# Attention in one fused post-norm block: the value sums of two key tiles issued back to back in the first query chunk

## The chip, the cores and the metric

The kernel runs on one core of a Trainium2 chip. The metric is the device time of one execution in microseconds (us), taken as the median of three runs. Smaller is better.

## What is computed

The reference is one transformer block with layer norms behind both halves. Its input is x, 4096 rows of 256 floats.

```
proj = quant4(x) @ ternary_weight(Wqkv).T + b
q = proj as (16 heads, 4096, 16);  k, v = proj read as (16, 4096, 16) in another order
q, k = rotary(q), rotary(k);   ql, kl = q @ U, k @ U
y = softmax(ql @ kl^T / 4) @ v            # for each head, 4096 x 4096
x1 = layernorm(x + quant4(y) @ ternary_weight(Wo).T)
h = silu(x1 w1) * (x1 w2);  h = gelu(h h1);  h = gelu(h h2)
out = layernorm(x1 + h w3)
```

The softmax is taken without subtracting a row's true maximum; a bound is folded into the scores, and a slower second attempt exists in the program for inputs on which that fails. It isn't run here.

## The kernel before, in words

**Work.** The attention is cut into 8 query chunks of 512 queries and, in each, 4 blocks of 4 heads. A block goes over 32 key tiles of 128 keys. One key tile for the 4 heads of a block is a **unit**, so a block has 32 units, a query chunk 128, and the whole attention 1024. The first query chunk is units 0 to 127.

**One unit** is three steps on three engines' worth of work:

- *Scores* (TensorE, `first_scores_pe`, L722): two **pairs**, each of two matmuls (one per head, 49 rows of contraction, 512 queries), which write two banks of PSUM. There are three such slots (`SLOTS`), used in turn by the pairs, so pair p + 3 can be computed only when pair p has been read.
- *Exponentials* (ScalarE, `first_act`, L812): one activation per pair, 128 x 1024, from PSUM into the ring `PB` of six places (`RING`).
- *Value sums* (TensorE, `first_sums_pe`, L752): 4 matmuls, one per head, with 17 columns of weights (16 values and a one), which add to one bank of PSUM, `ACC`. [...] The last one frees two places of `PB` (`probs_free`).

At the end of a block VectorE transposes `ACC` into `accS` (L1027) and divides; TensorE waits for that (`acc_saved`) ahead of the next block's first sums.

**Order.** TensorE's order is written out by hand in `first_pe`. For each unit: the scores of the pairs three ahead, each behind a wait for the activation that frees its slot; then at most one **setup step**; then the unit's value sums.

```
                for pair in IN_UNIT[unit]:
                    if pair + SLOTS < len(ACT_PAIRS):
                        pe.wait_ge(at["probs_ready"], pair + 1)
                        first_scores_pe(pe, at, pair + SLOTS)
```

**Setup steps.** Keys and queries of later rows are prepared in the gaps of the first chunk. The table `SETUP_AT` says at which unit which step stands: `XT` (L464) and `PR` (L469) turn and project a group of 512 rows, `KT` and `QT` (both L475) turn the rotated keys and queries, `KG` (L479) multiplies keys by U, `KN` and `QN` (L484) take norms, `KM` (L487) turns a maximum. All of them share one bank of PSUM, the last, and each waits until VectorE has read the one before it (`setup_read`). In units 6 to 127 they stand at these units:

- KT and KT at 16 and 17, 34 and 35, 48 and 49, 66 and 67, 80 and 81; KG and KG at the two units behind each of these pairs (18 and 19, 36 and 37, 50 and 51, 68 and 69, 82 and 83)
- PR and PR at 10 and 11, 42 and 43, 74 and 75, 25 and 26, 57 and 58
- KN then XT at 22 and 23, 40 and 41, 54 and 55, 72 and 73; KN alone at 7 and 86; XT alone at 9; KM at 24, 56 and 88
- QT and QT at 98 and 99, 108 and 109, 118 and 119; QN at 103, 113 and 123

KT, KG and KG's second step belong to one group of rows; units 1 and 2 hold a KT each and units 3 and 4 a KG each. ScalarE puts one more activation (`sqk` L526 or `sqq` L531) into its order behind the unit two behind the second KG or QT.

**Later chunks.** From block 7 on, in four units of each block half of the exponentials are made by VectorE (L823 to L839); the sums of these late units stand behind the sums or scores of other units (`LATE_AT`). That of unit 25 of a block stands directly behind the sums of unit 30. After the attention come the output projection and the feed-forward part.

Of the kernel before, what the change touches and what calls it, by code (L numbers as in the profile page):

```python
# [22 lines left out]
KT = N // P  # L23
# [8 lines left out]
NBLK = H // BL  # L32
# [57 lines left out]
LATE_NUMBER = {_u: _k for _k, _u in enumerate(LATE)}  # L90
# [45 lines left out]
def postln_block(nc, a, out):  # L136
    ctx = ExitStack()
    with ctx:
# [569 lines left out]
        def first_scores_pe(pe, at, pair):  # L708
            unit, s = ACT_PAIRS[pair]
            b, kt = divmod(unit, KT)  # L710
            q, k = divmod(unit, KQ)
            if s == 0 and k == 0:
                pe.wait_ge(at["k_in"][q % 2], keys_in(at, 0, q))
                if q < 2:
                    pe.wait_ge(consts_first[q], 64)
            if unit == 0 and s == 0:
                pe.wait_ge(q_first, 64)
            elif s == 0 and kt == 0:
                pe.wait_ge(at["q_in"][b % 2], (b // 2 + b % 2) * 64)
            for e in range(2):  # L720
                r = slice(64 * e, 64 * e + at["rows"])
                ins = pe.matmul(PS[:, 2 * (pair % SLOTS) + e, :], KSL[r, q % 2, s, k * P:(k + 1) * P],  # L722
                                QSL[r, b % 2, s, :], start=True, stop=True, tile_position=(64 * e, 0))
            ins.then_inc(at["scores_ready"], 1)

        def late_scores_pe(pe, at, unit, e):

            n = LATE_NUMBER[unit]
            b = unit // KT
            q, k = divmod(unit, KQ)  # L730
            pe.wait_ge(at["k_in"][q % 2], keys_in(at, 0, q))
            if n == 0 and e == 0:
                pe.wait_ge(setup_read, len(USE))
            else:
                pe.wait_ge(poly_read, 2 * n + e)
            r = slice(64 * e, 64 * e + at["rows"])
            pe.matmul(MISC, KSL[r, q % 2, 1, k * P:(k + 1) * P], QSL[r, b % 2, 1, :], start=True, stop=True,  # L737
                      tile_position=(64 * e, 0)).then_inc(poly_scores, 1)

        def first_sums_pe(pe, at, unit):  # L740
            hb, kt = unit // KT % NBLK, unit % KT
            c, u = divmod(kt, HT)
            if unit in LATE_NUMBER:
                pe.wait_ge(poly_ready, LATE_NUMBER[unit] + 1)
            pe.wait_ge(at["probs_ready"], IN_UNIT[unit][-1] + 1)
            for i in range(BL):
                h = hb * BL + i
                if unit in LATE_NUMBER:
                    probs = (late_act, late_dve)[i // 2][LATE_NUMBER[unit] % 2]
                else:  # L750
                    probs = PB[:, (2 * IN_RING[unit] + i // 2) % RING, :]
                ins = pe.matmul(ACC[i * VW:i * VW + DK + 1, :], V17[:, HT * h + u, c, :],  # L752
                                probs[:, (i % 2) * QW:(i % 2 + 1) * QW],
                                start=kt == 0, stop=kt == KT - 1, tile_position=(0, i * VW))
            ins.then_inc(late_free if unit in LATE_NUMBER else at["probs_free"], 1)

        def first_pe(pe, at):
            def place(unit, n):
                for what, late in PLACES.get((unit, n), []):
                    if what == "sums":  # L760
                        first_sums_pe(pe, at, late)
                    else:
                        late_scores_pe(pe, at, late, what)

            pe.wait_ge(setup_read, len(BEFORE))
            for pair in range(SLOTS):
                first_scores_pe(pe, at, pair)
            visits = {FIRST_Y: ("Y", 0)}
            for k in range(2):
                visits[FIRST_O[k]], visits[FIRST_X[k]] = ("O", k), ("X", k)  # L770
            for unit in range(NB_ALL * KT):
                place(unit, 0)
# [4 lines that stand above are left out]
                    if pair == IN_UNIT[unit][0]:  # L777
                        place(unit, 1)
                if unit in SETUP_AT:
                    setup_pe(pe, *SETUP_AT[unit])  # L780
                n = unit - KT * (NB_ALL - 1)
                if n == FIRST_Y:
                    pe.wait_ge(poly_read, 2 * len(LATE))
                if n in visits:
                    first_chunk_pe(pe, *visits[n], 0)
                if n == FIRST_W:
                    pe.wait_ge(fx1T_split, 2)
                    pe.wait_ge(least_weight, 1)
                    pe.transpose(MISC[0:1, 0:P], sm[:, 5, 1:2], ident[:, :]).then_inc(weights_T, 1)
                place(unit, 2)  # L790
                if unit % KT == 0:
                    pe.wait_ge(at["acc_saved"], unit // KT + 1)
                if unit not in LATE_NUMBER:
                    first_sums_pe(pe, at, unit)
                place(unit, 3)

        def first_act(act, at):
# [121 lines left out]
        def first_chunk_pe(pe, what, k, r):  # L919
            if what == "Y":  # L920
                pe.wait_ge(fy_ready, r + 1)
                for i in range(TQ):
                    for c in range(DC):
                        ins = pe.transpose(MISCB[:, i * DC + c, :], first_qb[:, i, c * P:(c + 1) * P], identb[:, :])
                ins.then_inc(fyT_ready, 1)
            elif what == "O":
                pe.wait_ge(fyT_saved, r + 1)
                if k:
                    pe.wait_ge(fo_read, 2 * r + 1)
                for i in range(2):  # L930
                    for c in range(DC):
                        ins = pe.matmul(MISC[:, i * D:(i + 1) * D], qTb[:, (2 * k + i) * DC + c, :], sgn[:, 1, c, :],
                                        start=c == 0, stop=c == DC - 1)
                ins.then_inc(fo_ready, 1)
            else:
                pe.wait_ge(fx1_ready, r + 1)
                if k:
                    pe.wait_ge(fx1T_split, 2 * r + 1)
                for i in range(TQ):
                    ins = pe.transpose(MISC[:, i * P:(i + 1) * P], yq[:, i, k * P:(k + 1) * P], ident[:, :])  # L940
                ins.then_inc(fx1T_ready, 1)
# [648 lines left out]
        def _(pe):  # L1590
# [22 lines left out]
            for v in BEFORE[1:]:  # L1613
                setup_pe(pe, *v)
            first_pe(pe, first)
            def again_pe(pe):
                maxima_pe(pe)
# [154 lines left out]
```

## Time and profile before

| What | Value |
|---|---|
| Median of 3 runs | 2587.75 us (2587.68 to 2589.11) |
| Profiled execution, its own time | 2590.94 us |
| Span of the trace | 2589.1 us |
| TensorE (matmul) busy | 2516.6 us, 97% |
| ScalarE busy | 2014.8 us, 78% |
| VectorE busy | 1740.3 us, 67% |
| First activation of the attention | at 66.72 us |
| Mean granted clock of TensorE | 0.991 of full speed |

Times in the trace count from the start of its span, and the profiled execution's own time is 1.8 us longer than that span. TensorE's matmuls overlap, so its share of busy time is no measure of how close it is to its limit. A row of a timeline merges neighbouring instructions of one kind: its start, its length from the first start to the last end, the count, and in brackets the idle time of that engine just ahead, with what ended it.

### The profile page before, as it was taken

How to read it: one execution, taken by the hardware profiler on the slowest of the kernel's cores; microseconds unless marked ns; L12 is line 12 of the kernel's file. 1: busy time of each engine (PE TensorE's matmuls, PEld its weight loads, DVE VectorE, ACT ScalarE, POOL GpSimd, SP SyncE). 2: the span in 40 equal slices, each digit the busy share in tenths (PEclk: the TensorE clock that was granted, in tenths of full speed). 3: DMA queues.
4: the chain of work that ended last, by engine and by line, in shares of the span. 5: the costliest groups of instructions: out<-in, count | busy, mean ns of one | idle time of the engine just before them, and what ended most of it. 6: DMA issues, size and time to landing. Idle time of an engine off the chain costs nothing.

```text
span 2589.1 us, 41403 instructions
## 1 busy us (share of the span) xinstructions
PE 2516.6 (97%) x15898; PEld 1094.7 (42%) x15898; DVE 1740.3 (67%) x2485; ACT 2014.8 (78%) x2230; POOL 40.4 (2%) x77
## 2 busy tenths in 40 slices
PE   3999999999999999999999999999999999999998
PEld 2222222222222222222222222222248888888886
DVE  7454345787787787887777877777644566646563
ACT  2899999999999999999999999999962223222232
POOL 1000001100000000000000000000100000000000
PEclk8999999999999999999999999999999999999999
DMA  3543447833343333243333334333630101110000
GB/s 106 122 103 88 109 115 158 167 62 70 59 77 71 68 64 71 58 76 71 66 65 71 59 75 73 63 68 72 122 63 1 25 0 24 24 24 16 8 8 18
DMA packets 100192, 172.27 MB, mean 67 GB/s; under 512 B 31208, under 2 KB 56840, under 8 KB 100014
## 3 DMA queue, kind: packets, MB, share of 16 engines
q1 hardware_dynamic: 89166, 151.84, 29.2%
q0 software_dynamic: 9120, 16.18, 3.1%
q8 instruction: 112, 1.84, 0.3%
q10 hardware_dynamic: 1728, 1.87, 0.3%
q14 instruction: 66, 0.54, 0.1%
HBM read 144.31 MB, written 25.49 MB: 66 GB/s over the span
## 4 chain that ended last, share of the span: by engine, by line
PE 85%; ACT 6%; issue 5%; DVE 3%; DMA 1%; ACTq 0%; SPq 0%; DVEq 0%
PE PS L752 33%; PE PS L722 24%; PE PS L1284 18%; ACT PB L812 5%; PE PS L1269 5%; PE PS L1296 2%; PE PS L737 2%; ACT EXP L812 1%; PE PS L475 1%; PE PS L479 1%; DMA wh1r<-in_mlp 0%; DVE yq L848 0%; DVE same L850 0%; PE PS L484 0%; PE PS L469 0%
## 5 line engine op out<-in xcount | busy, mean ns | idle before, releaser
L812 ACT ACTIVATE PB<-PS 128x1024 f32<-128x1024 f32 x1856 | 1734.5, 1139 | 38.0 <-PE PS L722 35.2
L752 PE MATMUL PS<-PB,V 128*17 128x512 f32 x7424 | 979.8, 600 | 3.5 <-DVE accS L1027 2.6
L722 PE MATMUL PS<-QSL,KSL 49*128 49x512 f32 x3904 | 838.0, 469 | 19.2 <-ACT PB L812 11.6
L722 PEld LDWEIGHTS PS<-QSL,KSL 49*128 49x128 f32 x3904 | 351.3, 184 | 937.5 <-ACT PB L812 851.0
L835 DVE SCALAR_TENSOR_TENSOR EXP<-EXP 128x1024 f32<-128x1024 f32 x288 | 352.8, 1225 | 9.9
L1363 ACT ACTIVATE hfr<-PS,s 128x512 f32<-128x512 f32 x128 | 86.9, 690 | 300.3 <-PE PS L1284 300.2
L752 PEld LDWEIGHTS PS<-PB,V 128*17 128x17 f32 x7424 | 123.2, 95 | 284.0 <-issue 217.4
L823 DVE TENSOR_SCALAR EXP<-PS 128x512 f32<-128x512 f32 x192 | 132.6, 691 | 157.0 <-PE PS L737 154.5
L1284 PE MATMUL PS<-hidden_ar,wh1r 128*128 128x512 f32 x1024 | 237.5, 391 | 0.0
L1284 PE MATMUL PS<-hidden_br,wh2r 128*128 128x512 f32 x1024 | 235.3, 390 | 0.0
L1284 PEld LDWEIGHTS PS<-hidden_br,wh2r 128*128 128x128 f32 x1024 | 191.7, 188 | 39.4
L1284 PEld LDWEIGHTS PS<-hidden_ar,wh1r 128*128 128x128 f32 x1024 | 190.7, 188 | 40.1 <-DVE hfr L1456 0.5
L1355 ACT ACTIVATE SLr<-PS,s 128x512 f32<-128x512 f32 x64 | 44.2, 691 | 122.1 <-PE PS L1269 122.1
L1269 PE MATMUL PS<-x1Tr,w12r 128*128 128x512 f32 x512 | 122.9, 400 | 2.3 <-issue 2.3
L1390 DVE CAST hidden_br<-hfr 128x512 fp32r<-128x512 f32 x64 | 27.3, 426 | 138.2 <-ACT hfr L1363 138.2
L832 DVE TENSOR_TENSOR EXP<-EXP 128x1024 f32<-128x1024 f32 x96 | 117.6, 1225 | 3.3
L839 DVE SCALAR_TENSOR_TENSOR EXP<-EXP 128x1024 f32<-128x1024 f32 x96 | 117.7, 1226 | 3.3
L827 DVE SCALAR_TENSOR_TENSOR EXP<-EXP 128x1024 f32<-128x1024 f32 x96 | 117.6, 1225 | 3.3
L1390 DVE CAST hidden_ar<-hfr 128x512 fp32r<-128x512 f32 x128 | 54.6, 426 | 94.8 <-ACT hfr L1363 92.5
L812 ACT ACTIVATE EXP<-PS 128x1024 f32<-128x1024 f32 x96 | 109.8, 1144 | 0.0
L1027 DVE STREAM_TRANSPOSE accS<-PS 128x512 f32<-128x512 f32 x32 | 22.9, 717 | 127.0 <-PE PS L752 126.7
L1269 PEld LDWEIGHTS PS<-x1Tr,w12r 128*128 128x128 f32 x512 | 94.1, 192 | 28.7 <-DVE hfr L1456 7.4
(184 smaller groups left out, 1463.8 us busy)
## 6 DMA issues: line engine op xcount, KB each, us to landing
KSL<-KSD SPq DMA_DIRECT2D x255, 256.0 KB
KSL<-KSD SPq DMA_DIRECT2D x255, 128.0 KB
QSD<-qhl SPq DMA_DIRECT2D x32, 256.0 KB
wh2r<-in_mlp POOLq DMA_DIRECT2D x32, 256.0 KB, 4.3
QSL<-QSD SPq DMA_DIRECT2D x62, 132.0 KB
KSD<-khl SPq DMA_DIRECT2D x58, 128.0 KB
xg<-in_x SPq DMA_DIRECT2D x8, 512.0 KB, 6.4
y<-Y SPq DMA_DIRECT2D x32, 128.0 KB, 2.2
```

What stands on the lines that cost most here:

```text
L722: ins = pe.matmul(PS[:, 2 * (pair % SLOTS) + e, :], KSL[r, q % 2, s, k * P:(k + 1) * P], QSL[r, b % 2, s, :], start=True, stop=True, tile_ ...
L752: ins = pe.matmul(ACC[i * VW:i * VW + DK + 1, :], V17[:, HT * h + u, c, :], probs[:, (i % 2) * QW:(i % 2 + 1) * QW], start=kt == 0, stop=k ...
L812: act.activation(probs, PS[:, slot:slot + 2, :].rearrange("p a b -> p (a b)"), ACT.Exp).then_inc(at["probs_ready"], 1)
L823: v.tensor_scalar(ey[:, e * QW:(e + 1) * QW], MISC, LOG2E, -126.0, ALU.mult, ALU.max).then_inc(poly_read, 1)
L827: s.did(v.scalar_tensor_tensor(ee, et, TO_WHOLE, ey, ALU.subtract, ALU.subtract))
L832: s.did(v.tensor_tensor(ey, ey, ee, ALU.mult))
L835: s.did(v.scalar_tensor_tensor(ey, ey, POW2[c], ee, ALU.add, ALU.mult))
L839: v.scalar_tensor_tensor(late_dve[k % 2], ey, POW2[0], et, ALU.add, ALU.mult).then_inc(poly_ready, 1)
L1269: ins = pe.matmul(PS[:, 2 * (o % 2) + w, :], w12[:, w, c, o * P:(o + 1) * P], x1p[:, r, c, :], start=c + r == 0, stop=c == DC - 1 and r == ...
L1284: ins = pe.matmul(PS[:, o % 4, :], wh[l - 1][:, c, o * P:(o + 1) * P], hidden[(l - 1) % 2][:, r, c, :], start=c + r == 0, stop=c == HC - 1 ...
L1363: act.activation(hf[:, o % FB, :] if exact else hidden[l % 2][:, 0, o, :], PS[:, o % 4, :], ACT.Gelu, scale=s12[:, 1 + l, o:o + 1]).then_i ...
L1390: sf.did(v.tensor_copy(parts[0], whole))
```

## The change

In units 0 to 127 an even unit issues no value sums. The odd unit behind it issues, after its own scores and its own setup step, the sums of the even unit and then its own. From unit 128 on nothing is changed.

```
                 place(unit, 2)
-                if unit % KT == 0:
-                    pe.wait_ge(at["acc_saved"], unit // KT + 1)
-                if unit not in LATE_NUMBER:
-                    first_sums_pe(pe, at, unit)
+
+                for ready in (unit,) if unit >= NBLK * KT else (unit - 1, unit) if unit % 2 else ():
+                    if ready % KT == 0:
+                        pe.wait_ge(at["acc_saved"], ready // KT + 1)
+                    if ready not in LATE_NUMBER:
+                        first_sums_pe(pe, at, ready)
                 place(unit, 3)
```

No instruction is added or removed, on any engine or queue. Only TensorE's order changes. The diff shifts the lines below it by two, so L812 becomes L814 and L1027 becomes L1029; L722 and L752 keep their numbers.

TensorE at the start of the attention (units 0 to 3; L722 are scores, L752 value sums, L475 and L479 setup steps), as one piece of the difference:

```order
-L722 MATMUL PS<-QSL,KSL 128x512 x10
-L752 MATMUL PS<-PB,V 17x512 x4
-L722 MATMUL PS<-QSL,KSL 128x512 x4
+L722 MATMUL PS<-QSL,KSL 128x512 x14
 L475 MATMUL PS<-ident,rk 128x128 x4
-L752 MATMUL PS<-PB,V 17x512 x4
+L752 MATMUL PS<-PB,V 17x512 x8
 L722 MATMUL PS<-QSL,KSL 128x512 x4
 L475 MATMUL PS<-ident,rk 128x128 x4
```

The sums of unit 0 moved behind the scores and the setup step of unit 1.

TensorE in units 16 to 19, where both KT and both KG steps of a group stand, before:

```order
L722 MATMUL PS<-QSL,KSL 128x512 x4
L475 MATMUL PS<-ident,rk 128x128 x4
L752 MATMUL PS<-PB,V 17x512 x4
L722 MATMUL PS<-QSL,KSL 128x512 x4
L475 MATMUL PS<-ident,rk 128x128 x4
L752 MATMUL PS<-PB,V 17x512 x4
L722 MATMUL PS<-QSL,KSL 128x512 x4
L479 MATMUL PS<-rkT,gblk 128x512
L752 MATMUL PS<-PB,V 17x512 x4
L722 MATMUL PS<-QSL,KSL 128x512 x4
L479 MATMUL PS<-rkT,gblk 128x512
L752 MATMUL PS<-PB,V 17x512 x4
```

and with the change:

```order
L722 MATMUL PS<-QSL,KSL 128x512 x4
L475 MATMUL PS<-ident,rk 128x128 x4
L722 MATMUL PS<-QSL,KSL 128x512 x4
L475 MATMUL PS<-ident,rk 128x128 x4
L752 MATMUL PS<-PB,V 17x512 x8
L722 MATMUL PS<-QSL,KSL 128x512 x4
L479 MATMUL PS<-rkT,gblk 128x512
L722 MATMUL PS<-QSL,KSL 128x512 x4
L479 MATMUL PS<-rkT,gblk 128x512
L752 MATMUL PS<-PB,V 17x512 x8
```

The two KG steps (L479) now have only four score matmuls between them, and 8 sum matmuls (16 records) follow behind the second.

## Rows read from the trace of the kernel before

**Rows 1.** The page: busy time by engine, share of the span, instructions.

```profile
PE 2516.6 (97%) x15898; PEld 1094.7 (42%) x15898; DVE 1740.3 (67%) x2485; ACT 2014.8 (78%) x2230; POOL 40.4 (2%) x77
```

**Rows 2.** Waits, 85 to 331 us: who waited for whom, total, times, longest.

```profile
ACT PB L812 <- PE PS L722: 12.7, 32, 0.8
...
PEld PS L752 <- DVE accS L1027: 0.9, 3, 0.3
```

**Rows 3.** Timeline of ScalarE: start, length, idle time ahead.

```profile
84.43 1.05 ACT L526 ACTIVATE sqk<-khl 128x1024 fp32r<-128x1024 f32 x1
85.38 10.30 ACT L812 ACTIVATE PB<-PS 128x1024 f32<-128x1024 f32 x11
...
250.05 28.51 ACT L812 ACTIVATE PB<-PS 128x1024 f32<-128x1024 f32 x31
```

**Rows 4.** Timeline of TensorE's matmuls, units 18 to 23.

```profile
108.92 0.73 PE L722 MATMUL PS<-QSL,KSL 49*128 49x512 f32 x4
109.58 1.12 PE L479 MATMUL PS<-rkT,gblk 128*128 128x512 f32 x2
110.64 1.05 PE L752 MATMUL PS<-PB,V 128*17 128x512 f32 x8
111.62 0.73 PE L722 MATMUL PS<-QSL,KSL 49*128 49x512 f32 x4
112.28 1.12 PE L479 MATMUL PS<-rkT,gblk 128*128 128x512 f32 x2
...
119.14 0.64 PE L484 MATMUL PS<-sqk,nbk 128*16 128x512 f32 x2
119.70 1.05 PE L752 MATMUL PS<-PB,V 128*17 128x512 f32 x8
```

**Rows 5.** Timeline of VectorE behind a KG, a KN and a KT step.

```profile
108.04 0.69 DVE L618 COPY rkT<-PS 128x512 f32<-128x512 f32 x1 [1.54 <-PE PS L475]
...
111.47 0.69 DVE L630 TENSOR_TENSOR khl<-PS,khl 128x512 fp32r<-128x512 f32 x1
...
119.88 0.68 DVE L638 TENSOR_REDUCE kmp<-PS 16x2 f32<-16x512 f32 x1 [1.52 <-PE PS L484]
```

**Rows 6.** Timeline of TensorE: KT (107 us) and PR (125 us), VectorE's read of PR.

```profile
107.35 0.66 PE L475 MATMUL PS<-ident,rk 128*128 128x128 f32 x4
107.94 1.05 PE L752 MATMUL PS<-PB,V 128*17 128x512 f32 x8
...
125.31 0.61 PE L469 MATMUL PS<-sgn,qTb 128*128 128x256 bf16 x4
125.84 1.05 PE L752 MATMUL PS<-PB,V 128*17 128x512 f32 x8
125.95 0.88 DVE L603 SCALAR_TENSOR_TENSOR xq<-PS,mx,alpha 128x256 f32<-128x256 f32 x2 [1.25 <-PE PS L469]
```

**Rows 7.** Timeline, 276 to 279 us: the second QT step and VectorE's reads.

```profile
276.68 0.65 PE L475 MATMUL PS<-ident,rq 128*128 128x128 f32 x4
...
278.10 0.69 DVE L630 TENSOR_TENSOR qhl<-PS,qhl 128x512 fp32r<-128x512 f32 x1
```

**Rows 8.** Timeline, 846 to 850 us: two units' sums in succession, in a later block.

```profile
846.08 0.50 PE L722 MATMUL PS<-QSL,KSL 49*128 49x512 f32 x2
846.51 1.05 PE L752 MATMUL PS<-PB,V 128*17 128x512 f32 x8
847.38 1.04 PE L752 MATMUL PS<-EXP,V 128*17 128x512 f32 x8
848.35 0.73 PE L722 MATMUL PS<-QSL,KSL 49*128 49x512 f32 x4
...
848.89 1.02 ACT L812 ACTIVATE PB<-PS 128x1024 f32<-128x1024 f32 x1
```

**Rows 9.** Timeline of TensorE, a pair of scores that waits for its slot.

```profile
86.45 0.50 PE L722 MATMUL PS<-QSL,KSL 49*128 49x512 f32 x2
```

**Rows 10.** Busy time by stretch: TensorE, its weight loads, VectorE, ScalarE, GpSimd, granted clock.

```profile
60.00:80.00 20.00, 13.73 (x64) 4.59 (x64) 7.76 (x12) 10.46 (x11) 1.47 (x4) 0.62 0.68 146
```

## The prediction

> **What bounds the kernel now.** I looked first at the busy times. TensorE shows 97% [rows 1], but its matmuls overlap, and the share says little. So I read who waits in the stretch that the change touches, the first query chunk. From 85 us to its end ScalarE waits for scores only 32 times, 12.7 us in all [rows 2]. Between these waits it runs without a break: 31 activations in 28.51 us, so that, with one of 1.02 us, the pitch is (28.51 - 1.02) / 30 = 0.916 us [rows 3]. ScalarE is the bound, and TensorE holds it up only where setup steps make a unit longer than two activations, 1.83 us: a unit with a KG takes 111.62 - 108.92 = 2.70 us [rows 4]. Each break costs ScalarE the gap that is shown and 1.02 - 0.916 = 0.105 us of lost overlap. The chunk before therefore loses 12.7 + 32 x 0.105 = **16.1 us** against an unbroken ScalarE.
>
> **What the change does to the time.** It gives no engine less to do. It makes TensorE's work coarser, and the point is how far ahead of ScalarE the scores are: three PSUM slots, so three pairs. I follow one round of two units (four pairs) from the last pair of scores of the odd unit to the same place in the next round.
>
> - That pair must wait until its slot is read. It starts 0.05 us after an activation's end: 85.38 + 1.02 = 86.40, against 86.45 [rows 3, 9].
> - Sums follow 846.51 - 846.08 = 0.43 us after its start. Two units' sums in succession take 0.87 and 0.97 us until scores start again, 848.35 - 846.51 = 1.84 us [rows 8]. The trace has this order once in each later block, so this is no guess.
> - The next pair of scores feeds an activation 848.89 - 848.35 = 0.54 us after its start. This activation is the one whose end frees the slot for the last pair of the next round. It takes 1.02 us, and 0.05 us later the round is closed.
>
> The round is 0.43 + 1.84 + 0.54 + 1.02 + 0.05 = **3.88 us**. Four activations need 4 x 0.916 = 3.66 us. So a round without any setup step, which costs ScalarE nothing now, will cost **0.22 us**. The cover that it had is gone: a single unit's sums, 111.62 - 110.64 = 0.98 us [rows 4], end 0.6 us before the scores behind them are needed; two units' sums end 0.22 us too late.
>
> A setup step in the *odd* unit stands inside this loop, between the last scores and the sums, and adds all its length. A step in the *even* unit stands beside ScalarE's waiting and adds nothing by itself. But if both units have one, the second needs the shared bank, which VectorE must first have read, and now only four score matmuls stand between the two steps, where sums stood as well. Such a round is counted from its first scores: 0.66 us to the even step (109.58 - 108.92 [rows 4]), then the time until the bank is free, then the odd step, then 1.84 us of sums. The bank is free (VectorE's end plus an estimated 0.09 us for the hand-over; after a KG TensorE goes on at most 0.12 us behind it, 112.28 against 112.16):
>
> - KT: 108.04 + 0.69 - 107.35 = 1.38, so 1.47 us; KN: 119.88 + 0.68 - 119.14 = 1.42, so 1.51; PR: 125.95 + 0.88 - 125.31 = 1.52, so 1.61 [rows 4 to 6].
> - KG, which VectorE reads twice: 111.47 + 0.69 - 109.58 = 2.58, so 2.67; QT likewise 278.10 + 0.69 - 276.68 = 2.11, so 2.20 [rows 4, 5, 7].
>
> The steps' own lengths are 0.59 (KT, and QT taken as that), 0.53 (PR, and XT taken as 0.55), 0.56 (KN) and 1.06 us (KG) [rows 4, 6]. From unit 6 to 127 there are 61 rounds. Their loss against 3.66 us:
>
> - 26 rounds with no step in the odd unit: 26 x 0.22 = 5.7
> - 7 with a short step in the odd unit that finds the bank free (units 7, 9, 25, 57, 103, 113, 123): 7 x (0.22 + 0.55) = 5.4
> - 5 KT with KT: 5 x (0.66 + 1.47 + 0.59 + 1.84 - 3.66 = 0.90) = 4.5
> - 4 KN with XT: 4 x (0.66 + 1.51 + 0.55 + 1.84 - 3.66 = 0.90) = 3.6
> - 3 PR with PR (units 10, 42, 74): 3 x (0.66 + 1.61 + 0.53 + 1.84 - 3.66 = 0.98) = 2.9
> - 3 QT with QT: 3 x (0.66 + 2.20 + 0.59 + 1.84 - 3.66 = 1.63) = 4.9
> - **5 KG with KG**: 5 x (0.66 + 2.67 + 1.06 + 1.84 - 3.66 = 2.57) = 12.9
> - 8 in which ScalarE has an extra activation of 85.38 - 84.43 = 0.95 us (L526, and L531 taken alike) [rows 3]: TensorE's delay is hidden, 0
>
> Together 39.9 us, where 16.1 are lost now: **23.8 us more**.
>
> The rest comes to nothing. In units 0 to 5 TensorE runs at a granted clock of 0.62 in the mean of its 20 us [rows 10]. The scores of unit 1 now come before the first, slow sums, which gains about 1.5 us; the KT and KG steps of units 2 and 3 give it back. I take 0 and keep 2 us on both sides, since the order of the work there could also move the moment at which the clock rises. The three waits for VectorE's transpose at block ends, 0.9 us [rows 2], disappear behind the second unit's scores, but they weren't on ScalarE's path and are worth 0. No DMA moves; the loads of keys are released by counts of scores and get more time, not less. Everything after unit 127 starts later by what the chunk lost.
>
> The profiled execution took 2590.94 us, 3.2 us over the median; the same difference on the median gives 2587.75 + 23.8 = **2611.5 us**.
>
> **A rule weighed.** Sums that follow sums cost 0.87 us where sums before scores cost 0.97 [rows 8]: 0.10 us saved. The Trainium skill, TensorEngine Tiling (Array Packing), Key Properties, says that a change of tiling mode drains TensorE, and scores (two row tiles) and sums (four column tiles) are different modes. The row agrees in direction, and by this rule the change should help; it halves the changes of mode. This case's rows decide what that is worth, below.
>
> **The rivals.**
>
> - *TensorE's work is what counts, and it gets shorter: faster.* If the first sums save 0.10 us and the scores side, for which there is no row, as much again, 64 rounds save 13 us of TensorE's time. What can be won is only where ScalarE waits now: 32 units in which TensorE is never idle, 16 rounds x 0.2 = 3 us, so about 2584; all of it gone would be 2587.75 - 16.1 = 2572. This decides if the sums of two units, with scores ahead and behind, fit into the three pairs of scores in hand, that is if 1.84 us were under 1.62. Rows 8 speak against it, the long chain through TensorE for it. Chance 0.05.
> - *No difference.* The waits gone in the odd positions and the new ones balance, if the KG rounds hide behind VectorE and the plain rounds cost nothing. 2587 to 2592. Chance 0.05.
> - *Slower, but the shared bank isn't felt.* VectorE reads sooner, or the second step stands late enough. Then KG with KG costs 0.66 + 1.06 + 0.66 + 1.06 + 1.84 - 3.66 = 1.62, QT 0.81, and the others 0.75 to 0.81: 8.9 us less, so 2602.7. Chance 0.15.
> - *Slower still.* The clock rises later at the start (2 us), and each of 53 rounds takes 0.05 to 0.1 us more than these rows say (3 to 5 us): 2617 to 2619. Chance 0.15.
>
> The forecast itself has 0.6. The range goes from 2602 to 2619. A measurement of this kernel tells about 0.2%, or 5.2 us, from no change. Faster by more than that 0.05, within it 0.05, slower 0.90.
>
> **What would show it.** In the trace after, between 85 us and the end of the chunk, ScalarE should wait for scores in some 53 places instead of 32; single waits of about 0.1 us in plain rounds (0.22 less the overlap), about 2.4 us at the five KG rounds. Units 16 to 19 should show the second L479 starting about 2.7 us after the first, with TensorE idle near 1 us ahead of it, waiting for VectorE's L630. Each two sets of sums should be 1.84 us. The time from unit 128 on should be unchanged. I am wrong if plain rounds keep 3.66 us, or if the second KG starts directly behind its scores.

## The result and the profile after

| | before | with the change |
|---|---|---|
| Median, first measurement | 2587.72 us | 2616.59 us (2615.83 to 2617.79, 4 runs) |
| Ratio, 95% interval | | 1.011 (1.0095 to 1.0125) |
| Median, second measurement (e9) | 2589.92 us | 2612.83 us (2611.69 to 2614.69, 4 runs) |
| Ratio, 95% interval | | 1.0092 (1.0075 to 1.0108) |
| Profiled execution of the first | 2590.94 us, span 2589.1 | 2617.79 us, span 2616.0 |

The change makes the kernel slower by 28.9 us in the first measurement and by 22.9 in the second. I had said 23.8. TensorE's clock is the likely reason why the two measurements differ; how far that is shown comes below.

The page of the kernel after, as in [rows 1]:

```profile
PE 2514.0 (96%) x15898; PEld 1101.5 (42%) x15898; DVE 1739.9 (67%) x2485; ACT 2019.4 (77%) x2230; POOL 40.1 (2%) x77
```

No engine has more to do. (The records count some matmuls twice: a unit's four matmuls of value sums are 8 records and a KG's one is 2, while the two of a pair of scores are 2.) The waits of ScalarE from 85 us to the end of the first chunk, now at 360 us (who waited for whom, total us, times, longest), answer to [rows 2]:

```profile
ACT PB L814 <- PE PS L752: 26.1, 27, 2.1
ACT PB L814 <- PE PS L722: 6.4, 27, 0.9
```

54 waits instead of 32, and 32.5 us instead of 12.7. Most is put down to the value sums (L752), which free the places of the ring `PB`, and not to the scores. The 54 are two in each of the 27 rounds with a step in the odd unit, one behind sums and one behind scores. The list leaves out the short waits of the plain rounds. They can be seen in ScalarE's timeline, where 18 activations at the pitch would take 17 x 0.916 + 1.02 = 16.59 us:

```profile
132.84 17.50 ACT L814 ACTIVATE PB<-PS 128x1024 f32<-128x1024 f32 x18 [0.18 <-PE PS L722]
```

The 0.91 us beyond that are four plain rounds with 0.23 us each, a gap of about 0.12 us and the lost overlap. TensorE in units 26 to 33, in its timeline (units 28 to 33 have no setup step):

```profile
134.34 1.91 PE L752 MATMUL PS<-PB,V 128*17 128x512 f32 x16
136.19 0.98 PE L722 MATMUL PS<-QSL,KSL 49*128 49x512 f32 x6
137.80 0.49 PE L722 MATMUL PS<-QSL,KSL 49*128 49x512 f32 x2 [0.64 <-ACT PB L814]
138.23 1.91 PE L752 MATMUL PS<-PB,V 128*17 128x512 f32 x16
140.07 0.99 PE L722 MATMUL PS<-QSL,KSL 49*128 49x512 f32 x6
141.69 0.51 PE L722 MATMUL PS<-QSL,KSL 49*128 49x512 f32 x2 [0.63 <-ACT PB L814]
142.12 1.91 PE L752 MATMUL PS<-PB,V 128*17 128x512 f32 x16
```

The loop of the prediction can be read off. The last pair of scores starts at 137.80, the sums 0.43 us later, scores again 1.84 us after that, and the next last pair at 141.69: a round of 3.89 us. TensorE itself waits 0.64 us in each for the slot to be read, and ScalarE 0.12 us for scores: both engines wait for each other in turn. The KG round of units 18 and 19, against [rows 4, 5], first TensorE:

```profile
113.28 1.12 PE L479 MATMUL PS<-rkT,gblk 128*128 128x512 f32 x2
114.34 0.73 PE L722 MATMUL PS<-QSL,KSL 49*128 49x512 f32 x4
115.92 1.12 PE L479 MATMUL PS<-rkT,gblk 128*128 128x512 f32 x2 [0.85 <-DVE khl L630]
116.97 1.91 PE L752 MATMUL PS<-PB,V 128*17 128x512 f32 x16
118.81 0.96 PE L722 MATMUL PS<-QSL,KSL 49*128 49x512 f32 x6
```

then VectorE's read of the bank:

```profile
115.17 0.69 DVE L630 TENSOR_TENSOR khl<-PS,khl 128x512 fp32r<-128x512 f32 x1
```

and ScalarE's activation behind the block:

```profile
118.15 1.02 ACT L814 ACTIVATE PB<-PS 128x1024 f32<-128x1024 f32 x1 [2.14 <-PE PS L752]
```

The second KG starts 2.64 us after the first, behind VectorE's second read, with 0.85 us of idling ahead of it.

I took the length of every round from the ends of its activations (from the last of one round to the last of the next; TensorE works three pairs ahead, so the round of units 6 and 7 is felt in the activations of units 8 and 9). The loss is what goes beyond 3.67 us, four times the pitch, and beyond the extra activation where there is one. Summed over units 6 to 127:

| Rounds | predicted | before | first profile | e9's profile |
|---|---|---|---|---|
| 26 without a step in the odd unit | 5.7 | 0.7 | 5.8 | 5.9 |
| 7 with one short step there | 5.4 | 0.7 | 10.3 | 5.5 |
| 5 KT with KT | 4.5 | 1.8 | 4.6 | 4.6 |
| 4 KN with XT | 3.6 | 1.2 | 3.1 | 3.1 |
| 3 PR with PR | 2.9 | 2.2 | 2.9 | 2.9 |
| 3 QT with QT | 4.9 | 1.1 | 4.8 | 4.8 |
| 5 KG with KG | 12.9 | 8.7 | 12.7 | 12.7 |
| 8 with an extra activation | 0 | -0.2 | -0.2 | -0.2 |
| Sum (rounding apart) | 39.9 | 16.1 | 44.0 | 39.3 |

The waits give the same sum another way: 32.5 us, 54 times 0.105 us of lost overlap, and 26 times 0.22 in the plain rounds are 43.9 us.

Only one line is far off in the first profile, and it is all in three rounds: those of units 102, 112 and 122, with a QN step, lose 2.4 us each and not 0.8. TensorE there, in the first profile:

```profile
302.32 0.50 PE L722 MATMUL PS<-QSL,KSL 49*128 49x512 f32 x2 [0.42 <-ACT PB L814]
302.76 1.02 PE L484 MATMUL PS<-sqq,nbk 128*16 128x512 f32 x2
303.71 3.13 PE L752 MATMUL PS<-PB,V 128*17 128x512 f32 x16
```

and in e9's, the same program executed again:

```profile
301.52 0.50 PE L722 MATMUL PS<-QSL,KSL 49*128 49x512 f32 x2 [0.42 <-ACT PB L814]
301.96 0.64 PE L484 MATMUL PS<-sqq,nbk 128*16 128x512 f32 x2
302.53 1.91 PE L752 MATMUL PS<-PB,V 128*17 128x512 f32 x16
```

The same matmuls take 3.13 us once and 1.91 the other time. The busy times of two stretches (TensorE, its loads, VectorE, ScalarE, GpSimd, then the granted clock), the fall and what came ahead of it in the first profile:

```profile
302.80:306.20 3.40, 3.40 (x16) 0.58 (x18) 2.39 (x4) 1.76 (x3) 0.00 (x0) 0.50 0.93 218
299.00:302.80 3.80, 2.96 (x21) 0.91 (x14) 0.00 (x0) 3.80 (x5) 0.00 (x0) 1.00 0.63 203
```

The granted clock is at half, 1.2 GHz, from 302.8 to 306.2 us, and so twice more. Ahead of it ScalarE runs off its reserve (scores that TensorE made in advance during the extra activation), and TensorE has only single pairs of scores to issue, 0.9 us apart. The cost is (2.40 + 2.41 + 2.43) - 3 x 0.8 = 4.8 us.

The profiled executions differ by 26.9 us. The rounds make 44.0 - 16.1 = 27.9 of it. The first activation came 0.8 us later (67.55 against 66.72), and from there to the end of unit 7 it took 0.15 us more. Units 130 to 135 lose another 0.5 us. Then 1.9 us come back at a block end near 457 us, and 0.8 us behind the attention. At that block end the profile of before shows a fall of the clock (457.7 us), the one after doesn't. The difference to before changes there by 1.6 us in e9's profile and 2.4 in e7's, which have no fall either, and by 0.1 in e4's, which has one at 481.9 us. By these figures the fall cost the profiled execution of before about 2 us, which has nothing to do with the change.

### The profile page after: what moved, and what is told of

It reads as the page before. It is cut to its first block, busy times and chain, and to the rows that moved or that the text cites. A ratio compares the mean times of both kernels' runs of the same rounds, so it can differ in the third digit from the quotient of the medians.

```text
span 2616.0 us, 41403 instructions
## 1 busy us (share of the span) xinstructions
PE 2514.0 (96%) x15898; PEld 1101.5 (42%) x15898; DVE 1739.9 (67%) x2485; ACT 2019.4 (77%) x2230; POOL 40.1 (2%) x77
## 3 DMA queue, kind: packets, MB, share of 16 engines
q8 instruction: 112, 1.84, 0.3%
## 4 chain that ended last, share of the span: by engine, by line
PE 76%; ACT 12%; issue 8%; DVE 3%; DMA 1%; ACTq 0%; POOL 0%; SPq 0%; DVEq 0%; POOLq 0%
PE PS L752 28%; PE PS L722 19%; PE PS L1286 18%; ACT PB L814 11%; PE PS L1271 5%; PE PS L1298 2%; ACT EXP L814 1%; PE PS L737 1%; PE PS L479 1%; PE PS L475 1%; DMA wh1r<-in_mlp 0%; DVE yq L850 0%; DVE same L852 0%; PE PS L469 0%; ACT sqk L526 0%
## 5 line engine op out<-in xcount | busy, mean ns | idle before, releaser
L814 ACT ACTIVATE PB<-PS 128x1024 f32<-128x1024 f32 x1856 | 1740.0, 1140 | 60.6 <-PE PS L752 29.2
L752 PE MATMUL PS<-PB,V 128*17 128x512 f32 x7424 | 970.5, 601 | 3.1 <-DVE accS L1029 2.2
L722 PE MATMUL PS<-QSL,KSL 49*128 49x512 f32 x3904 | 837.9, 469 | 41.4 <-ACT PB L814 33.9
L722 PEld LDWEIGHTS PS<-QSL,KSL 49*128 49x128 f32 x3904 | 352.7, 184 | 930.1 <-ACT PB L814 820.8
L752 PEld LDWEIGHTS PS<-PB,V 128*17 128x17 f32 x7424 | 130.2, 95 | 303.3 <-issue 241.7
L1029 DVE STREAM_TRANSPOSE accS<-PS 128x512 f32<-128x512 f32 x32 | 22.9, 716 | 133.5 <-PE PS L752 133.2
L814 ACT ACTIVATE EXP<-PS 128x1024 f32<-128x1024 f32 x96 | 110.3, 1149 | 0.0
```

The lines of the kernel that those rows point to most:

```text
L814: act.activation(probs, PS[:, slot:slot + 2, :].rearrange("p a b -> p (a b)"), ACT.Exp).then_inc(at["probs_ready"], 1)
```

## Experiments

The experiments ran on three chips. All times are set against the kernel before as measured on the same chip beside them: 2589.02 us for e1 to e4, 2588.65 for e5 to e8, 2589.92 for e9.

**e1: pair only where the odd unit has no step.**

```
-                for ready in (unit,) if unit >= NBLK * KT else (unit - 1, unit) if unit % 2 else ():
+                round_of = unit // 2 * 2
+                paired = unit < NBLK * KT and round_of + 1 not in SETUP_AT
+                for ready in (unit,) if not paired else (unit - 1, unit) if unit % 2 else ():
```

> The sums are paired only in the 34 rounds whose odd unit has no setup step; elsewhere they stand as before. Theory (three pairs of scores in hand, two units' sums end 0.22 us too late): each plain round costs ScalarE 0.22 us, rounds with the extra activation nothing, and where a round ahead of setup steps has lost its reserve the first step there costs up to 0.45 us more; in sum 8.5 us over before, 2596, no drop of TensorE's clock in the first chunk. Rival 1 (every pairing costs alike, 28.9 us / 64 = 0.45 us each): 34 x 0.45 = 15 us, 2603. Rival 2 (fewer changes of tiling mode help, only setup steps hurt): at or under 2587.7, plain rounds at 3.66 us.

Measured: 2596.97 us, 8.0 over before (1.0031, 1.0019 to 1.0044). The 26 plain rounds lose 0.22 or 0.23 each, the 8 rounds with an extra activation nothing, the unpaired KG rounds 1.73 to 1.74 as before, and the KT and QT rounds 0.80 instead of 0.35, the lost reserve. Their sum is 24.7, 8.6 over before, and I had expected 8.5. TensorE goes from the one form to the other in its timeline:

```profile
136.03 0.49 PE L722 MATMUL PS<-QSL,KSL 49*128 49x512 f32 x2 [0.64 <-ACT PB L816]
136.46 1.91 PE L752 MATMUL PS<-PB,V 128*17 128x512 f32 x16
138.30 0.99 PE L722 MATMUL PS<-QSL,KSL 49*128 49x512 f32 x6
139.92 0.51 PE L722 MATMUL PS<-QSL,KSL 49*128 49x512 f32 x2 [0.63 <-ACT PB L816]
```

A round of 139.92 - 136.03 = 3.89 us, without any setup step near. Both rivals fall. With 0.45 us for every pairing it would be 2603 us, which lies above the interval, and 8 of the 34 pairings cost nothing. And where TensorE changes its mode half as often, no round is faster.

**e2: the same pairings, the other parity.**

```
-                for ready in (unit,) if unit >= NBLK * KT else (unit - 1, unit) if unit % 2 else ():
+                for ready in (unit,) if unit >= NBLK * KT - 1 or unit == 0 else (unit - 1, unit) if unit % 2 == 0 else ():
```

> As many pairings as in the change, but a round is an odd unit and the even unit behind it, so that the two KG steps, and the two QT steps, fall into different rounds. Theory: a KT first and a KG second costs 1.37 us, a KG first 0.56 us and that is hidden behind the extra activation, QT with KT's length 0.8 us instead of 1.6; against that the three block ends now fall inside a round (the second sums wait for VectorE's transpose), 1.3 us each instead of 0.22; in sum 16 us over before, 2604, and no clock drop in the QN rounds. Rival (the number of pairings or the doubled sums alone decide, the shared bank does not): the same time as with the change, 2616.6.

Measured: 2607.65 us, 18.6 over before (1.0069, 1.0052 to 1.0086). The change has 28.9 and 22.9; the interval of the second (from 1.0075) still touches this one, so the rounds have to decide. They lose 31.8 us together, against 39.3 in e9's profile, which has no fall of the clock in the attention either. That is 15.7 over before, with 1.25 or 1.26 at each of the three block ends; I had expected 16 in all. The start of the attention loses 2.4 us more (the last activation of unit 7 ends at 89.67 instead of 87.31), which wasn't in my 16. TensorE in units 17 to 20:

```profile
111.26 0.66 PE L475 MATMUL PS<-ident,rk 128*128 128x128 f32 x4
111.85 0.87 PE L722 MATMUL PS<-QSL,KSL 49*128 49x512 f32 x4
112.76 1.13 PE L479 MATMUL PS<-rkT,gblk 128*128 128x512 f32 x2
113.82 1.91 PE L752 MATMUL PS<-PB,V 128*17 128x512 f32 x16
115.66 0.73 PE L722 MATMUL PS<-QSL,KSL 49*128 49x512 f32 x4
116.32 1.12 PE L479 MATMUL PS<-rkT,gblk 128*128 128x512 f32 x2
```

The second KG (116.32) now has a double block of sums ahead of it and no wait for VectorE, and the QT rounds go from 1.59 to 0.81. So the shared bank is one term of the change's price, and the parity decides it.

**e3: late sums, but not in succession.** The edit is shown against the kernel with the change. `sums_of` issues one unit's sums, with its wait.

```
                    if pair == IN_UNIT[unit][0]:
                        place(unit, 1)
+                        if unit < NBLK * KT and unit % 2:
+                            sums_of(unit - 1)
...
-                for ready in (unit,) if unit >= NBLK * KT else (unit - 1, unit) if unit % 2 else ():
+                for ready in (unit,) if unit >= NBLK * KT or unit % 2 else ():
+                    sums_of(ready)
```

> In the odd unit the even unit's sums stand between its two pairs of scores, and its own sums at the end: the sums are as late as in the change but no two follow each other. Theory: what costs is the length of the double block; plain rounds go back to 3.66 us (0 lost), the reserve for a step in an odd unit is 0.15 us instead of 0.65, so setup rounds lose somewhat more than before; in sum 8.5 us over before, 2596. Rival (it is the even unit's late sums, which free the ring of exponentials late): plain rounds lose 0.22 us as in the change, 2610 or more.

Measured: 2597.94 us, 8.9 over before (1.0036, 1.0023 to 1.0048). The plain rounds are back at 0.00 us of loss (0.37 in two that lost 0.35 before), and the rounds with one step in the odd unit lose 0.42 to 0.47 instead of 0.77 (0.18 at unit 9). What costs is the length of the block, not that the even unit's sums come late. They come one pair of scores earlier here than in the change; the ring, which they free, is taken up in e4.

**e4: the change with eight places for exponentials.** The two added places lie in `first_y` and `first_x`, free until unit 972; behind unit 127 there are six again.

```
+        def place_number(n):
+            return n % 8 if n < 2 * NBLK * KT else n % RING
...
-                    if n >= RING:
-                        act.wait_ge(at["probs_free"], (n - RING) // 2 + 1)
-                    probs = PB[:, n % RING, :]
+                    if n in BEFORE_IT:
+                        act.wait_ge(at["probs_free"], BEFORE_IT[n] // 2 + 1)
+                    probs = place_of(n)
```

> The change, with eight places for exponentials instead of six in the first chunk (the two added places lie in tensors that are not used until much later). The profile puts 26 us of ScalarE's waits in the first chunk down to the value sums, which free the ring. Theory (three PSUM slots for scores end the round): these waits go, but the scores are not earlier, so every round keeps its length: 2616.6, within 1 us. Rival (the ring of six is what binds): the waits for sums go and the time falls by 10 to 26 us, 2591 to 2607.

Measured: 2616.98 us, 28.0 over before (1.0109, 1.0092 to 1.0126). Waits of ScalarE in the first chunk:

```profile
ACT PB L829 <- PE PS L722: 17.8, 15, 2.4
ACT first_x L829 <- PE PS L722: 12.8, 12, 2.4
ACT PB L829 <- PE PS L767: 1.7, 1, 1.7
```

27 waits for sums have become one (1.7 us, where the ring shrinks again), and the rounds are where they were: 0.22, 0.92 and 2.53 us of loss, with waits for scores in their place. In its profile every round of the first chunk is within 0.02 us of the same round in e9's, save the last, which loses 1.76 us instead of 0.22 as the ring shrinks. This profiled execution has no fall of the clock in the first chunk and took 2615.27 us. The median lies higher because of two others, which took 2618.7 and 2618.9 us and have no trace. The profile's 26 us "for L752" were true and without consequence. In the change's own KG round the activation held by the ring starts at 118.15 and the next, held by scores, at 119.35: 1.20 us on, 0.28 more than the pitch of 0.92. So the scores would have held the second of the two 0.28 us longer than the ring held the first, and with the ring taken away they still hold the round.

**e5 and e6: where the fall of the clock comes from.** The edit is that of e1 with other conditions: `round_of + 1 not in (99, 101, 109, 111, 119, 121)` and `round_of + 1 not in (103, 113, 123)`.

> The change, but with the sums unpaired in the three rounds with both QT steps and the three rounds behind them (units 98 to 101, 108 to 111, 118 to 121). The change's profile showed TensorE's granted clock fall to half in the QN rounds that follow (3 stretches of 3.4 us, 1.65 us lost in each beyond the ledger). Theory (it is the idling in the QT rounds, where TensorE waits 0.7 us for VectorE and then for ScalarE's extra activation, that brings the clock down): QT rounds lose 0.35 us instead of 1.59, the clock stays up, the QN rounds lose 0.79 us; 3.7 us under the change from the rounds and up to 5 more from the clock: 2608 to 2613. Rival (the drop belongs to the QN round and its doubled sums): the drop stays, QN rounds at 2.4 us.

> The change, but with the sums unpaired in the three QN rounds (units 102 and 103, 112 and 113, 122 and 123). Theory (the drop of the clock comes from what TensorE did ahead of them): the drop is still there, since it begins at the QN step, and the QN rounds lose 1 us or more; the time is 0 to 3 us under the change, 2614 to 2617. Rival (the drop is made by the doubled sums in that round): no drop, these rounds lose nothing, 2.4 x 3 = 7 us under the change, 2609.

Measured: e5 2612.12 us, 23.5 over before (1.0093, 1.0078 to 1.0109), e6 2609.16 us, 20.5 over before (1.0079, 1.0063 to 1.0094). In e5's profile the QT rounds lose 0.80 each (not 0.35, since the plain round ahead had used up the reserve, as in e1), and the clock still falls in two of the three QN rounds, which lose 2.2 and 2.4 us. My theory that the waits in the QT rounds bring it down is refuted. e6's profile has no fall in the attention, and its QN rounds lose nothing. That fitted the rival, but e9 takes the proof away again.

**e9: the change once more.**

> The change itself once more, on the chip that runs it now. Open is whether TensorE's drop to half clock in the QN rounds (4.9 us beyond the ledger in the first profile; absent in the profile of the change with a ring of eight) comes in every execution. Theory (it comes in some, as the QN rounds leave TensorE with single pairs of scores for some 3 us and the drop depends on how they fall): executions spread over about 5 us, those with a mean granted clock of 0.991 or more near 2612 to 2615, those of 0.990 and less near 2616 to 2619. Rival (it is fixed in the order of the work): all within 1 us of 2617, with the same clock.

Measured: 2612.83 us, 22.9 over before, and in its profile no fall of the clock in the attention; this is the program whose first profile had three. So the fall comes in one execution and not in another. In e9 the stretch ahead of the QN step has the same busy times as the one that I showed above:

```profile
298.00:301.80 3.80, 2.96 (x20) 0.86 (x12) 0.00 (x0) 3.80 (x5) 0.00 (x0) 1.00 0.63 194
301.80:305.20 3.40, 3.40 (x26) 0.97 (x24) 2.57 (x5) 2.82 (x4) 0.00 (x0) 1.00 0.87 224
```

2.96 us of TensorE and 3.80 of ScalarE in 3.80, in both. I found nothing in the rows that tells the two apart. The theory on e9 was borne out in that executions can differ, but not in that they spread within one measurement: all four of e9 were alike (2611.69 to 2614.69, mean clock 0.991 and 0.992), and all four of the first lie above them (2615.83 to 2617.79, 0.989 to 0.991). The rival, all near 2617, is refuted. A difference between chips isn't excluded by this, but e4's four, on one chip, fell into 2613.5 and 2615.3 with 0.991 and 2618.7 and 2618.9 with 0.990. What decides it stays open.

**e7 and e8: a version that beats both.** Without pairing, only the sums of a unit with a KG step go behind the first pair of scores of the next unit, and the first QT step stands two units earlier.

The edit is shown against the kernel before:

```
-    SETUP_AT.update({_u: (QT_, 0, _g), _u + 1: (QT_, 1, _g), _u + 5: (QN, 0, _g)})
+    SETUP_AT.update({_u - 2: (QT_, 0, _g), _u + 1: (QT_, 1, _g), _u + 5: (QN, 0, _g)})
...
+            late_sums = {u for u, v in SETUP_AT.items() if v[0] == KG}
...
                    if pair == IN_UNIT[unit][0]:
                        place(unit, 1)
+                        if unit - 1 in late_sums:
+                            sums_of(unit - 1)
...
+                if unit not in late_sums:
+                    sums_of(unit)
```

e8 has in addition other units for the steps (XT, PR, PR, KT, KT, KG, KG, KN): 8, 11, 12, 16, 17, 18, 19, 22, then 23, 25, 26, 30, 32, 35, 37, 40, then 41, 43, 44, 48, 49, 50, 51, 54, then 57, 58, 60, 64, 65, 67, 68, 72, then 74, 75, 76, 80, 81, 82, 83, 86.

> A version of the kernel before that uses what was learned: no pairing. Only the sums of a unit with a KG step are moved behind the first pair of scores of the next unit, so that the long step no longer delays that pair; and the first QT step of a group stands two units earlier, so that the reserve grows back between the two. Theory (what counts is how early the next scores are, three pairs in hand): the rounds with KG lose 1.3 us instead of 1.73, the QT rounds nothing instead of 0.35 (seven of them, four behind unit 127); 4.3 us under the kernel before, 2584 to 2585. Rival (later sums free the ring later, or more changes of mode cost TensorE more): no gain, or slower by 1 to 3 us.

> As the run before it, and the steps of the later groups of rows are spread further apart (a unit without a step between the PR, KT and KG steps where their order allows it). Theory: another 2.2 us from the reserve that grows back by 0.18 us in each unit without a step; 6.5 us under the kernel before, 2582 to 2583. Rival: VectorE, whose chain between the steps gets less time, makes TensorE wait, and the gain is lost.

Measured: e7 2584.51 us, 4.1 under before (0.9983, 0.9974 to 0.9992); e8 2582.24 us (2581.89 to 2583.6, 9 runs), 6.4 under before (0.9976, 0.9966 to 0.9985). In e8, TensorE in units 18 and 19:

```profile
109.35 1.12 PE L479 MATMUL PS<-rkT,gblk 128*128 128x512 f32 x2
110.41 0.49 PE L722 MATMUL PS<-QSL,KSL 49*128 49x512 f32 x2
110.83 1.05 PE L752 MATMUL PS<-PB,V 128*17 128x512 f32 x8
111.82 0.50 PE L722 MATMUL PS<-QSL,KSL 49*128 49x512 f32 x2
112.25 1.12 PE L479 MATMUL PS<-rkT,gblk 128*128 128x512 f32 x2
```

and ScalarE's waits in the first chunk:

```profile
ACT PB L819 <- PE PS L722: 7.0, 23, 0.5
```

The pair of scores goes ahead of the sums, 1.06 us behind the KG's start instead of 2.04 [rows 4]. The KG rounds lose 0.95 us instead of 1.73 in e7, where I had expected 1.3. But some rounds behind them lose more than before: KN with XT 0.56 instead of 0.30. The whole chunk loses 14.0 us in e7 and 11.4 in e8, against 16.1. Of the rest, 0.6 us (0.3 in e8) come from the start, where two KG steps stand as well, and 1.2 from the QT steps behind unit 127.

## Why the prediction was right, and where not

- *ScalarE is the bound and is held up through three pairs of scores.* Shown: e1 and e3 change only the place of the sums, and with it the block's length, and give the round lengths of the loop; e4 excludes the ring.
- *A plain round costs 0.22 us.* Measured 0.22 to 0.23, in 26 rounds of each profile with pairing.
- *A step in the odd unit adds its length, in the even unit nothing.* 0.77 to 0.79 in the rounds at full clock.
- *The second step waits for the bank* (measured against predicted). KG 2.53 against 2.57, QT 1.59 against 1.63, KT 0.92 against 0.90, PR 0.97 against 0.98. KN with XT measured 0.78 against 0.90: there the bank wasn't felt. I had allowed it 1.51 us, but in the profile after, VectorE's read of the KN's sums ends at 125.05 us, and the scores that go ahead of the XT are held by ScalarE until 125.03 and take until 125.47, where the XT starts: the bank was free by then.
- *The start gives nothing.* 0.15 us.
- *Everything from unit 128 on keeps its time.* Not quite: units 130 to 135 lost 0.5 us, and 0.8 us came back behind the attention. That these two nearly cancel is luck.
- *What the trace would show.* I named waits for scores in 53 places, one in each of 53 rounds. That 54 are listed is a coincidence: they are two in each of 27 rounds, half of them, and the long ones, stand against the sums, and with the short ones of the 26 plain rounds there are 80. The prediction followed the slots alone and didn't see that the activation ahead of the one it followed waits for the ring. e4 shows that this changed no round.
- *The clock.* The term that I had at nothing is the QN rounds' fall: 4.8 us in the profiled execution of the first measurement. I had put 2 us on the clock, at the start only. It would account for nearly all of the 5.1 us between 28.9 and 23.8, but that is argued and not shown: the other three executions have no trace, and the profiled ones differ by 26.9 us and not 28.9. In e9, without it, the time is 22.9 us over before, and the rounds give 39.3 - 16.1 = 23.2. How near the first measurement came to the forecast was therefore also up to the execution.
- *The rival of the bank that isn't felt.* Refuted: the second KG waits 0.85 us for VectorE's read, and the KG rounds lose 2.53 us and not 1.62.
- *The rival of the shorter TensorE.* Sums behind sums do save 0.1 us, 0.87 against 0.97 in [rows 8], but TensorE idles 0.64 us in the same round, so it is worth nothing here. The Trainium skill, TensorEngine Tiling (Array Packing), Key Properties, says that a change of the tiling mode drains TensorE. The two rows agree with it; no run here separates the drain from other causes of the 0.1 us.

## What to carry to other kernels

If a producer works N buffers ahead of the engine that bounds the kernel, look at the longest block that it issues between two fills, not only at its sum of work: add up the loop from one slot's release to the same slot's next release and compare it with N buffers' worth. Here grouping like work made the block longer and used up a reserve that irregular steps lived on, and moving the fill ahead of the long step's sums (e7) gained 4.1 us instead. A wait put down to one resource isn't the bound until it is taken away and the time moves.

## What the hardware showed that I had not expected

The granted clock of TensorE fell to half for 3.4 us at a time in the middle of the attention, three times in one execution of a program and in none of another of the same program, after a stretch in which TensorE was busy 2.96 of 3.80 us in both. Each cost the round about 1.6 us: 1.22 in the doubled block of sums (3.13 us instead of 1.91) and 0.38 in the QN step ahead of it (1.02 instead of 0.64), which both lie in the loop.
